# One window later: where the attention of a graph network multiplies weights by counts, and how its tile loop addresses the key tables

## The reference

```
h = x @ W                                    # [3125, 128]
score = leaky_relu(h[dst]·a1 + h[src]·a2, 0.2)
e = exp(clip(score, -2, 2))
alpha = e / (segment_sum(e, dst)[dst] + 1e-7)
x = layernorm(x + segment_sum(h[src] * alpha, dst))
# second layer: message MLP over the edges, mean by node, update MLP, residual, layernorm
```

## Time and profile before

| | |
|---|---|
| median of 3 runs | 2087.48 us |
| profiled execution, whole | 2091.26 us |
| its span in the profile | 2089.4 us |
| setup of tables | 0 to about 59 us |
| attention, 25 blocks of counts | about 60 to 857 us |
| node tables and message layer | from there to the end |
| busy in the whole span | PE 1704.9 (82%), PEld 1471.7 (70%), DVE 1578.3 (76%), ACT 1246.3 (60%), POOL 1157.0 us (55%) |

### The profile page before, as it was taken

One profiled execution on the slowest core, in us unless ns is written; L12 is line 12 of the kernel. 1 busy time (PEld: TensorE's weight loads), 2 busy tenths in 40 slices (PEclk: granted clock), 3 DMA queues, 4 the chain that ended last, 5 costly groups with the idle time before them and its releaser, 6 DMA issues.

```text
span 2089.4 us, 54564 instructions
## 1 busy us (share of the span) xinstructions
PE 1704.9 (82%) x15385; PEld 1471.7 (70%) x15386; DVE 1578.3 (76%) x3406; ACT 1246.3 (60%) x2301; POOL 1157.0 (55%) x1189
## 2 busy tenths in 40 slices
PE   4467777766666667562899999999999999999986
PEld 3345666655555555520799999999999999999974
DVE  4578878766555566742788888888888888888886
ACT  3014566667777777233566766666666666666651
POOL 3212355445555545110777777777777777777730
PEclk9799998888887888766899999999999999999999
DMA  2112333433344444113544445444444444455421
GB/s 73 30 37 70 93 104 109 114 109 114 111 120 121 124 117 122 40 63 108 158 138 139 138 137 138 139 137 138 140 139 138 138 139 138 138 138 139 137 60 31
DMA packets 138294, 235.98 MB, mean 113 GB/s; under 512 B 24569, under 2 KB 89165, under 8 KB 138230
## 3 DMA queue, kind: packets, MB, share of 16 engines
q0 software_dynamic: 49632, 142.89, 24.2%
q1 hardware_dynamic: 88598, 92.44, 15.1%
HBM read 185.52 MB, written 10.66 MB: 94 GB/s over the span
## 4 chain that ended last, share of the span: by engine, by line
PE 51%; DVE 1%; ACT 0%; issue 0%; DMA 0%; DVEq 0%; SPq 0%
PE ps L1207 9%; PE ps L1206 9%; PE ps L1212 9%; PE ps L1190 8%; PE psA L1224 6%; PE ps L1185 4%; PE ps L1198 4%; PE ps L946 1%; PE ps L957 0%; PE ps L954 0%; PE psA L965 0%; DVE x L1018 0%; ACT u L979 0%; DMA bias<-in_L_gnn_bm 0%; DVE stats L1029 0%
## 5 line engine op out<-in xcount | busy, mean ns | idle before, releaser
L1161 POOL DMA_INDIRECT ga<-table_a,idx x784 | 778.6, 993 | 240.3 <-issue 181.0
L1206 PE MATMUL ps<-wm_hi,h_hi 128*128 128x256 f32 x1568 | 422.4, 303 | 0.2 <-ACT h_hi L1257 0.2
L1261 ACT ACTIVATE h<-ps 128x512 bf16<-128x512 f32 x392 | 234.1, 597 | 285.6 <-PE ps L1212 285.6
L1207 PE MATMUL ps<-wm_lo,h_hi 128*128 128x256 f32 x1568 | 386.2, 280 | 0.0
L514 POOL DMA_INDIRECT head_n<-scr_eye,row_at x250 | 290.4, 1162 | 140.8 <-POOL row_at L510 99.1
L1347 DVE SCALAR_TENSOR_TENSOR rest<-ps,h 128x512 f32<-128x512 f32 x392 | 269.6, 688 | 123.6 <-ACT h L1261 120.9
L1206 PEld LDWEIGHTS ps<-wm_hi,h_hi 128*128 128x128 f32 x1568 | 294.5, 188 | 23.6 <-ACT h_hi L1257 1.2
L1207 PEld LDWEIGHTS ps<-wm_lo,h_hi 128*128 128x128 f32 x1568 | 295.4, 188 | 1.5
L557 PE MATMUL psC<-ring_n,ring_m 128*126 x1180 | 242.6, 339 | 53.8 <-DVE ring_n L680 29.6
L611 ACT ACTIVATE stage<-psC 126x626 f32<-126x626 f32 x125 | 86.2, 689 | 303.5 <-PE psC L566 301.1
L1341 DVE SCALAR_TENSOR_TENSOR h_lo<-ps,h_hi 128x512 fp32r<-128x512 f32 x392 | 264.5, 692 | 2.3 <-ACT h_hi L1257 2.3
(11 more groups left out here) (188 smaller groups left out, 2749.2 us busy)
## 6 DMA issues: line engine op xcount, KB each, us to landing
cnt<-stage SPq DMA_DIRECT2D x125, 305.2 KB
dstb<-scr_dst SPq DMA_DIRECT2D x196, 126.0 KB
ga<-table_a,idx POOLq DMA_INDIRECT x784, 2.9
bw<-table_b SPq DMA_DIRECT2D x196, 63.0 KB
table_b<-b_st SPq DMA_DIRECT2D x12, 375.0 KB
head_n<-scr_eye,row_at POOLq DMA_INDIRECT x250, 4.1
table_a<-a_st SPq DMA_DIRECT2D x12, 250.0 KB
x<-in_x SPq DMA_DIRECT2D x1, 1562.5 KB
```

What stands on the lines that cost most here:

```text
L1161: pool.indirect_dma_start(ga[:, u, k, :], None, table_a, bass.IndirectOffsetOnAxis(ap=idx[:, u, k:k + 1], axis=0)).then_inc(gathered[u][k] ...
L1206: pe.matmul(ps2[q][:, t % 2, :], hi, w_hi[:, k, :], start=False, stop=True, skip_group_check=True)
L1207: pe.matmul(ps2[q][:, t % 2, :], hi, w_lo[:, k, :], start=False, stop=True, skip_group_check=True)
```

## The change

Four things change together. (1) `WEIGH_AT` goes from (1, 3) to (2, 4): both parts of the multiplication by counts stand one window later. `LEAKY_AT` goes from (1, 2) to (1, 3): the second leaky part stands one window later. `BANKS_AT` starts the sums of a pair one window later, with two chunks after the pair's eighth window instead of one after the fourth. (2) DVE's tile loop counts in the shifted tables: for odd starts the counter begins 789 higher, and both tables are addressed by it without further arithmetic. For this, row 2 of `edge_keys`, whose content has been copied away, gets the column keys shifted by one. (3) The iota is stored once for each of 126 rows and repeated by a stride of zero. (4) Two large iotas at the start give way to one of 630 elements.

```diff
-BANKS_AT = (0, 0, 0, 1, 1, 1, 1, 1, 2, 2)
+BANKS_AT = (0, 0, 0, 0, 1, 1, 1, 2, 2, 2)
-WEIGH_AT = (1, 3)
-LEAKY_AT = (1, 2)
+WEIGH_AT = (2, 4)
+LEAKY_AT = (1, 3)
...
-                                             (T.iota_m[:, :, :, :], [[WM, WPB], [1, WM + 1], [0, TPT]], 0, 0),
-                                             (T.iota_h[:, :, :, :], [[WM, WPB], [1, WM + 1], [0, HEAD]], 0, 0)):
+                                             (T.iota_m[:, :, :], [[WM, WPB], [1, WM + 1]], 0, 0)):
...
+            step(dve.tensor_copy(T.edge_keys[:, 2, 0:KEYS - 1], T.edge_keys[:, 1, 1:KEYS]))
...
-                    with eng.Fori(first + HEAD, end, TPT) as n:
-                        n = bounded(n, HEAD, TILES - 1 + HEAD)
+                    low, high = first + HEAD, end
+                    if shifted:
+                        odd = eng.snap((low & 1) * (KEYS - 1), min_val=0, max_val=KEYS - 1)
+                        low, high = low + odd, high + odd
+                    with eng.Fori(low, high, TPT) as n:
+                        n = bounded(n, HEAD, TILES - 1 + HEAD + (KEYS - 1 if shifted else 0))
...
+            src_keys = T.edge_keys[:, 1:3, :].rearrange("p c n -> p (c n)")
+
             def hot_rows(at, n, v, u, tiles):
-                keys = block_keys[:, (v + 1) % 2, bass.ds(n + (n & 1) * (KEYS - 1), tiles)].rearrange("p (o s) -> p o s", o=1)
-                iota = T.iota_m if tiles == TPT else T.iota_h
-                return dve.tensor_tensor(at, iota[:, u, :, :], keys.broadcast_to([P, WME, tiles]), ALU.is_equal)
+                keys = block_keys[:, (v + 1) % 2, bass.ds(n, tiles)].rearrange("p (o s) -> p o s", o=1)
+                iota = T.iota_m[:, u, :].rearrange("p (m o) -> p m o", o=1)
+                return dve.tensor_tensor(at, iota.broadcast_to([P, WME, tiles]), keys.broadcast_to([P, WME, tiles]), ALU.is_equal)
...
-                hot_rows(head_m[:, w % 2, :, :], first, v, u, HEAD).then_inc(head_ready, 1)
+                hot_rows(head_m[:, w % 2, :, :], first + (first & 1) * (KEYS - 1), v, u, HEAD).then_inc(head_ready, 1)
...
-                                      T.edge_keys[:, 1, bass.ds(n + s, 1)], None, ALU.is_equal).then_inc(ring_ready[s], 1)
+                                      src_keys[:, bass.ds(n + s, 1)], None, ALU.is_equal).then_inc(ring_ready[s], 1)
```

More of the change, by code:

```diff
@@ L258, in _ @@
             step(dve.tensor_copy(T.src_idx[:, :], T.edge_keys[:, 2, 0:TILES]))
+            step(dve.tensor_copy(T.edge_keys[:, 2, 0:KEYS - 1], T.edge_keys[:, 1, 1:KEYS]))
             step(dve.memset(T.n_idx[:, TILES:KEYS], 0))
             step(dve.tensor_copy(T.n_idx[:, 0:TILES], T.edge_keys[:, 1, 0:TILES]))
-            dve.wait_ge(iota_done, 8)
+            dve.wait_ge(iota_done, 7)
             dve.wait_ge(range_back, 48)
@@ L453, in window_loads, with windows @@
             return load, tiles
-        def windows(eng, tag, head, tile, after):
+        def windows(eng, tag, head, tile, after, shifted):
             turn = eng.alloc_register(f"{tag}_turn")
@@ L568, in after @@
                 last.then_inc(window_summed, 1)
-            blocks(pe, windows(pe, "pe", head, tile, after))
+            blocks(pe, windows(pe, "pe", head, tile, after, False))
             for c in range(CH):
@@ L691, in after @@
                     add_chunk(t, v, c)
-            blocks(dve, windows(dve, "dve", head, tile, after))
+            blocks(dve, windows(dve, "dve", head, tile, after, True))
             for part in range(2):
@@ L1443, in sb_early @@
                 return early.enter_context(nc.sbuf_tensor(name, shape, dt))
-            T.iota_m = sb_early("iota_m", [P, WPB, WM + 1, TPT], i16)
-            T.iota_h = sb_early("iota_h", [P, WPB, WM + 1, HEAD], i16)
+            T.iota_m = sb_early("iota_m", [P, WPB, WM + 1], i16)
             T.n_idx = sb_early("n_idx", [P, KEYS], i32)
```

## The result

| | before | changed |
|---|---|---|
| median (range) | 2088.02 us (2086.47 to 2095.15) | 2120.21 us (2106.39 to 2128.26) |
| ratio, 95% interval | 1 | 1.0147 [1.011, 1.0184] |
| profiled execution, span | 2091.26, 2089.4 us | 2124.15, 2122.4 us |

The changed kernel is slower by 32 us (1.5%); the forecast was 30 us faster. In the traces everything behind the attention takes as long as before (from the last add into `acc` to the end 1205.8 and 1206.1 us), so the 33 us lie in the attention.

What follows compares the result with a forecast made beforehand. It took waits between engines in order to set the end, no engine being close to full. The terms -64.3 + 27 - 7.3 + 0 - 12 + 13 + 14 + 0.6 gave -29 us, so 2058 us; range 2045 to 2071.

Steps and rivals of the forecast that it cites:

- term 1: DVE's wait for the counts at weigh goes away because weigh stands after window 2: -64.3 us.
- term 4: Second leaky part and sums of a pair, moved later, cost nothing: 0 us; 36 if ACT's cover were gone.
- term 2: DVE's first leaky part now waits for ACT's relu: +27 us, with ends 0 and 50.
- rival A: DVE's wait only changes its name; PE and ACT come no earlier, relu's wait is 50: 2081 us, chance 0.17.
- 3, weigh in the shadow of the loop's end: Weigh's second part runs while DVE's sequencer stands at the loop's branch, five times: -7 us.
- 5, registers in the loop: Each step of DVE's loop saves 82 ns of register work in 145 sequencer-bound steps: -12 us.
- 6, registers between head and loop: Added DVE register operations cost 0.19 us in each of 68 exposed windows: +13 us.
- 7, the zero stride: DVE's compares with a zero-stride iota each take 0.12 us longer, 118 of them exposed: +14 us.
- Rival D: All 420 slower compares are exposed because DVE is the path through every window: 2094 us, chance 0.12.
- 8, the start: One copy of 789 elements on DVE's chain of setup at the start: +0.6 us.

Runs made afterwards that it cites:

- e11: Kernel before with only the three tables of places changed (weigh, leaky part, chunk sums) and four gather buffers: ratio 0.9876 to the kernel before, -26 us.
- e18: Same kernel as e11, run again in another job: ratio 0.9891 to the kernel before, -27 us.
- e9: The changed kernel run again unchanged: ratio 1.0131 to the kernel before, +27 us.
- e5: Changed kernel with four gather buffers in place of two: ratio 0.9917 to the kernel before, -20 us.
- e12: Kernel before with the changed order, the shifted loop and four gather buffers, without the zero stride: ratio 0.9888 to the kernel before, -23 us.
- e1: Kernel before with only the three tables of places changed (order alone): ratio 1.0048 to the kernel before, +10 us.
- e16: Same kernel as e1, run again in another job: ratio 1.0041 to the kernel before, +10 us.
- e3: Kernel before with only the loop changed, counting in the shifted tables: ratio 1.0049 to the kernel before, +10 us.
- e15: Order alone plus two more register operations between head and loop and a longer step: ratio 1.0216 to the kernel before, +53 us.
- e8: Changed kernel with the chunk sums at their old places: ratio 1.0049 to the kernel before, +12 us.
- e6: Kernel before with four gather buffers in place of two: ratio 0.9942 to the kernel before, -14 us.
- e4: Changed kernel without the zero stride, so order and loop change: ratio 1.0161 to the kernel before, +34 us.
- e10: Changed kernel with weigh and the leaky part in pieces of 625 columns: ratio 1.0149 to the kernel before, +31 us.
- e13: Changed kernel with weigh and the leaky part replaced by one-input reductions over the same columns: ratio 1.003 to the kernel before, +7 us.

## Why the prediction was wrong

**The step that failed** is that the 64.3 us of term 1 were booked as time, while the chain of gathers behind PE's head had no term and term 4 put the sums of a pair at 0. The order (terms 1 to 3) was to give 45 us and cost 10. With four buffers, where no wait for gathers is left, it gives 12 to 15. The rest is the size of term 2: with the relu's wait as measured there (58.4 us in e11, 54.5 in e18) terms 1 to 3 give -13 and -17. This agreement may be partly luck, since other waits moved as well. Loop and stride (terms 5 to 8) were to cost 16 us; on top of the order they cost 17 to 22.

**1, the wait for counts, -64.3.** Right as a wait: it is gone. Wrong as a gain: PE's wait for DVE's head and DVE's wait for the counts were one delay seen twice, and under it ran the gathers. What DVE saved came back in part as PE's wait for gathers, 53.1 to 92.5 us, and as DVE's own wait at the first add.

**2, the relu, +27.** Mis-sized: 45.6 us, and 49.7 in e9, the 50 of rival A. ACT's chain did not come earlier. Rival A gave PE's gathers as the reason, and that is not it: without any wait for gathers the relu's wait is 46.7 us in e5, 49.0 in e12 and 58.4 in e11, so the reason stays open. A gave 2081, 39 us short of what came: it had the right size of the wait and not the cause of the loss.

**3, weigh in the shadow of the loop's end, -7.** About right: over the five turns the stop ahead of `head_m` falls from 23.3 to 17.5 us (e1: 15.6, e16: 18.3). The turn shown here is one that did not shorten (5.07 us, and 4.81 in the earlier trace rows):
```profile
647.02 1.45 DVE L661 TENSOR_TENSOR pr<-pr,cnt 125x1250 f32<-125x1250 f32 x1
648.39 0.75 DVE L642 TENSOR_TENSOR acc<-psO,acc 125x387 f32<-125x387 f32 x2
654.21 0.55 DVE L673 TENSOR_TENSOR head_m<-iota_m,block_keys 128x378 bf16<-128x378 int16 x1 [5.07 <-issue]
658.41 0.42 DVE L673 TENSOR_TENSOR ring_m<-iota_m,block_keys 128x252 int16 x1 [3.64 <-issue]
```
The last line is new: a second stop, 3.64 us, behind the first head of the turn. Such stops at a `ring_m` stand in every kernel with more registers between head and loop (longest 4.2 us in e3, 5.2 in e12, 5.6 in e15); in those without, none is over 1 us. No term had them. e12, which has them, is within 2.5 us of e11, so by themselves they are not the loss; with two buffers they may be what loop and order lose together.

**4, the sums of a pair, 0.** Wrong. I wrote that the chunks moved "lie where DVE would wait for the relu". Of the four that moved, only chunk 2 does (behind window 1 of a pair's second block), and no add waits there, before or after. Chunk 0 went from behind window 3 to the first add, behind window 4, where DVE has nothing to wait for but PE. `acc`'s wait doubled (31.7 to 63.5 us), and e8, with the chunks back, is 15 to 20 us better. Asking who forms the sum at that place, and what stands ahead of it in PE's order, would have led to the gathers. The other half of the term held: ACT's cap shows no wait for DVE.

**The chain that no term had.** Release by PE, POOL's copy, two issues and the landing, with two buffers. The earlier trace rows showed 53.1 us of it, the second largest of PE's waits, and I used it only as the reason behind rival A; the text named its growth as what would make the forecast wrong, and gave it no price of its own. It grew by 39 us where DVE's wait lost 64. e5, e6, e11 and e12 show that two buffers are what turned the change into a loss: with four the same change is worth -6 us (e5 against e6, less than their intervals resolve), and the order alone -12 to -15.

**5, registers in the loop, -12.** The step did shorten by 0.05 us (1.23 to 1.17 or 1.18), but only while the ring fills. Then it is 1.22 to 1.26. From 84 to 112 us PE's idle before a ring matmul is 10.3 us of "issue" and 0.5 for DVE's `ring_n`, where before it was 7.5 us for `ring_n`: the limit has gone over to PE's own sequencer. Blocks 0 to 3 take 209.4 us (before: 209.5): terms 5 and 7 came to nothing together.

**6, registers between head and loop, +13.** The size was taken too large: in e3 the first compare behind a head comes only 0.05 us later (646 to 697 ns), and with the 0.08 us that the step's own registers lost this makes 0.13, near the 0.12 counted from the rows and under the 0.19 taken. Yet e3 costs +10 (5 to 16) for the loop as a whole, where terms 5 and 6 had +1. The second stops behind the turns, 16.7 us together in e3, are the likely rest; no run tests them alone.

**7, the zero stride, +14.** The durations are as forecast, 419 and 549 ns for 290 and 417, so the Trainium skill's rule on an innermost step of one (the page and section of the prediction) holds here. The cost in time is 7.5 us (2 to 13) alone and about nothing in the changed kernel (+34 without the zero stride in e4, +32 and +27 with it). Rival D falls with it: the slower side came, but not by its mechanism.

**8, the start, +0.6.** The first `head_m` starts at 62.65 us, 0.26 later than before. No run tests it further.

Sum: terms 1, 3 and 7 were right as events on DVE, and term 7's cost came only without the new order. The forecast fell because I took DVE for the path and let the time follow it.

## What to carry to other kernels

When two engines wait in turn, a wait of 64 us that is passed on to the other engine is worth at most what the other has left behind it: before counting a removed stop as gain, take every other wait of the engine that was served late (here PE's 53 us for gathers) and ask what it will be when that engine comes earlier. A prefetch with two buffers whose chain (here 3.4 us of issuing and a landing) is as long as a short window (3.0 to 3.9 us in the table) has no slack; more buffers cost memory and a few semaphores, and should be tried ahead of moving work about. An instruction that is moved to a later place drags along the engine that feeds it, and the add of a partial sum belongs behind the point at which its producer, in its own order, is sure to have reached it.

## What the runs showed of the hardware

- POOL's issue of an indirect DMA takes 0.95 to 0.97 us alone and up to 4.2 beside DVE's two-input instructions on SBUF. Of the 234 issues of the changed kernel from 100 to 850 us, the 155 that lie beside neither weigh nor the leaky part take 1.02 us in the mean, and the 12 that lie beside them for 1.5 us or more take 3.2. Cutting a long instruction into pieces that follow one another does not let POOL in (longest issue 4.6 us in e10).
- Compares in which one input (the iota) has a stride of zero innermost took 419 in place of 290 ns (252 elements) and 549 in place of 417 (378 elements in rows of three).
- DVE's sequencer, at the turn of a long loop body, stops for 3.5 to 6.4 us before and 2.0 to 5.1 in the changed kernel, and in the kernels with more registers between head and loop again a few instructions on (1.6 to 5.3 us in the changed kernel).
- The same program takes 2087 us in some jobs and 2465 to 2498 us, 18 to 20% longer, in others; all of the difference lies behind the attention. What differs is not shown: the record gives the chips of e9 to e12 (2087 us) and of e13 to e16 (2465 us) the same number.
